# Moving pairwise products between SBUF partitions: 0/1 matmuls or DMA, in a recommendation tower on one core

## The chip, the cores and the metric

The kernel runs on one core of one Trainium2 chip. The metric is the device time of one execution in microseconds, and less is better. Besides it there is a profile of one execution, with its own time.

## The reference

For 512 samples there are 27 feature vectors of 128 numbers: the given bottom output and 26 rows looked up in embedding tables by `ids`. The 351 dot products of all pairs of features, with the bottom output behind them, go through three layers:

```python
e = jnp.stack([tbl_0[ids[:, 0]], ..., tbl_25[ids[:, 25]]], axis=1)
all_emb = jnp.concatenate([bottom_output[:, None, :], e], axis=1)
gram = jnp.einsum('bfd,bgd->bfg', all_emb, all_emb)
z = gram[:, _TRIU_I, _TRIU_J]                       # 351 pairs of a sample
h = jnp.concatenate([z, r_bottom_output], axis=1)   # 479 columns
h = jnp.maximum(h @ W_top1 + b_top1, 0.0)           # 512 columns
h = jnp.maximum(h @ W_top2 + b_top2, 0.0)           # 256 columns
return h @ W_top3                                   # one number a sample
```

All is fp32. The kernel gets that accuracy from matmuls of a high and a low part of each operand, so a product costs three matmuls: high by high, high by low, low by high.

## The kernel before, in words

The samples are four tiles of 128. Instructions are put on each engine by hand, in a written order, and engines wait for one another by semaphores alone. There is no planner: the order of calls at the end of each engine's function is the order of its work.

Up to about 53 us nine small tables are looked up by matmuls with one-hot rows (lines 653 to 675). Rows of the other 17 tables are gathered by POOL with indirect DMA (line 283), five "banks" of up to four features for each tile, into `emb`, which holds two tiles. TensorE turns a bank with four transposes (`transpose_bank`, line 531); VectorE and ScalarE in turn copy it from PSUM into `embT` (`copy_bank`, lines 293 and 409).

For a tile t the work then is this:

- `gram(t, half)` (line 545): for each half of the tile 64 small matmuls, one for each sample, which are 128 in the trace, since an fp32 matmul of this kind takes two passes; four samples stand side by side on 32 PSUM partitions each. A sample's 26 columns of products land in `pG`.
- `copy_rows` (line 216): ScalarE copies the first half, VectorE the second, into `rows`. Here the partition is 32 times the sample's place among four, plus the feature; along a partition lie the other feature and 32 groups of samples.
- `turn(t)` (line 560): layer 1 wants pairs on partitions and samples along the row. Ten turns (`TURNS`, line 34) pack the triangle of pairs into three tiles of 127 rows, and for each of four sample groups a matmul with a 0/1 matrix `sel` moves the rows of one turn to their partitions: 40 matmuls by the code, 80 in the trace. The result is in PSUM and `products(t)` (line 210) names it.
- `high_products` (ScalarE, line 444) and `low_products` (VectorE, line 296) split it into `prod_hi` and `prod_lo`.
- `layer1_bottom` and `layer1_products` (lines 569, 570, 577): three matmuls for the bottom output and nine for the products; `relu` (line 459), `transpose_h1` (line 623), `high_h1` and `low_h1` (lines 466, 296), `layer2` (lines 634, 569, 570, 577), and `layer3` on VectorE (line 331).

`products(t)` of all tiles shares one `prod_hi` and one `prod_lo`, so the next tile's split waits for `s_l1`, the end of the layer 1 before. `rows`, `pG` and `emb` have two places each. TensorE's written order weaves tile t's layers with tile t+1's transposes and gram, so that something can run while ScalarE and VectorE copy. Tile 3 comes last and has its layer 1 in two parts.

SP issues all table and weight loads (lines 230, 236, 247), then waits for `s_y` and writes the output (line 265).

Of the kernel before, what the change touches and what calls it, by code (L numbers as in the profile page):

```python
# [33 lines left out]
TURNS = [(range(24 - 3 * n, 27 - 3 * n), 0, 26 - 3 * n, n if n < 4 else 7 - n, 0 if n < 4 else 32 - 26 + 3 * n - 1)  # L34
         for n in range(8)] + [(range(1, 3), 0, 1, 0, 31), (range(2, 3), 1, 1, 1, 31)]
LAST_TURN = {j: n for n, (_, _, _, j, _) in enumerate(TURNS)}
BIAS_QUADRANT, BIAS_ROW = 3, 31
N1, N2 = 512, 256
K2 = N1 // 128
# [28 lines left out]
def tower(nc, bottom, ids, hot_ids, tables, w1, w2, b2, w3, out):  # L68
# [4 lines left out]
    with ctx:  # L73
        def sb(name, shape, dt=fp32):
            return ctx.enter_context(nc.sbuf_tensor(name, shape, dt))
# [4 lines left out]
        def sem(name):  # L80
            return ctx.enter_context(nc.semaphore(name))
# [17 lines left out]
        bot_lo = sb("bot_lo", [128, TILES, 128], fp32r)  # L99
        sel = sb("sel", [128, len(TURNS), 4, 32])  # L100
        rows = sb("rows", [128, 2, COLS, GROUPS])
        prod_hi = sb("prod_hi", [128, KTILES, 128], fp32r)
        prod_lo = sb("prod_lo", [128, KTILES, 128], fp32r)
        w_hi = sb("w_hi", [128, CHUNKS, N1], fp32r)
# [34 lines left out]
        s_sel0 = sem("s_sel0")  # L139
        s_sel = sem("s_sel")  # L140
        s_prod1 = sem("s_prod1")
        s_row = [[sem(f"s_row{t}_{k}") for k in range(len(BANKS))] for t in range(TILES)]
        s_tabhi = sem("s_tabhi")
        s_tablo = sem("s_tablo")
# [64 lines left out]

        def products(t):  # L210

            return pG[t % 2][:, 0, 0:KTILES * 128].rearrange("r (k p) -> r k p", p=128)

        def copy_rows(copy, t, half):
# [11 lines left out]
        @block.sync  # L226
        def _(sp):
            def load_table(i, p0, p1, k0, k1, loaded):

                sp.dma_start(tab[p0:p1, i % RING, k0:k1, :], tables[LOOKED_UP[i]].rearrange(  # L230
                    "(p k) d -> p k d", k=VK)[p0:p1, k0:k1, :]).then_inc(loaded, 16)

            def load_lookup(i):
                if i >= RING:
                    sp.wait_ge(s_look, (i - RING + 1) * VK)
                sp.dma_start(hot[:, i % RING, :], hot_ids[i:i + 1, :].broadcast_to([128, B])).then_inc(s_hotids[i], 16)
                load_table(i, 0, VP_MAIN, 0, VK, s_tab[i])
                load_table(i, VP_MAIN, VP, 0, VK, s_tab[i])

            def load_weights(c):  # L240
                sp.wait_ge(s_look, (LOOKED - RING + c // 2 + 1) * VK)
                if c <= KTILES:
                    dst, src = chunk(c), w1[:, c, :]
                else:
                    dst = chunk(c).rearrange("p (k n) -> p k n", n=N2)
                    src = w2.rearrange("(k p) n -> p k n", p=128)[:, 2 * (c - KTILES - 1):2 * (c - KTILES), :]
                sp.dma_start(dst, src).then_inc(s_w[c], 16)

            sp.dma_start(idx[:, :], ids.rearrange("(p t) f -> p (t f)", t=TILES)).then_inc(s_ids, 16)
# [12 lines left out]
            for c in range(CHUNKS):  # L262
                load_weights(c)
            sp.wait_ge(s_y, TILES)
            sp.dma_start(out.rearrange("(p t) o -> p (t o)", t=TILES), y[:, :]).then_inc(s_out, 16)
            sp.wait_ge(s_out, 16)
# [22 lines left out]
        def _(dve):  # L289
# [8 lines left out]
            def low_products(t, part=None):  # L298
                ks = slice(0, KTILES) if part is None else (slice(0, 1), slice(1, KTILES))[part]
                if t > 0:  # L300
                    dve.wait_ge(s_l1, t)
                else:
                    dve.wait_ge(s_prod1, 2)

                dve.wait_ge(s_phi, t + 1 if part is None else t + 2)
                subtract(prod_lo[0:127, ks, :], products(t)[0:127, ks, :], prod_hi[0:127, ks, :]).then_inc(s_plo, 1)

            def second_rows(t):
                dve.wait_ge(s_gram, 2 * t + 2)
                if t >= 2:  # L310
                    dve.wait_ge(s_turn, t - 1)
                copy_rows(nc.vector.tensor_copy, t, 1).then_inc(s_rowsv, 1)

            def low_weights(c0, c1):
# [21 lines left out]
            nc.vector.memset(ones[:, :], 1.0).then_inc(s_ones, 1)  # L336
            nc.vector.memset(embT_flat[:, TILES * 128 * FEATURES:], 0.0).then_inc(s_pad, 1)
            nc.vector.memset(prod_lo[:, :, :].bitcast(fp32), 0.0).then_inc(s_prod1, 1)
            nc.vector.memset(sel[:, :, :, :], 0.0).then_inc(s_sel0, 1)
            dve.wait_ge(s_row0, 1)  # L340
            nc.vector.tensor_copy(row0f[:, :], row0[:, :]).then_inc(s_row0f, 1)
# [31 lines left out]
            subtract(b2_lo[:, :], b2s[:, :], b2_hi[:, :]).then_inc(s_b2, 1)  # L373

            copy_bank(1, 1)
            low_weights(2, 3)
            second_rows(0)
            low_weights(3, CHUNKS)
            copy_bank(1, 3)
            low_products(0)  # L380
            second_rows(1)
            low_h1(0)
            layer3(0)
            low_products(1)
            copy_bank(2, 0)
            copy_bank(2, 2)
            low_h1(1)
            copy_bank(2, 4)
            layer3(1)

            second_rows(2)
            low_products(2)
            copy_bank(3, 1)
            low_h1(2)
            layer3(2)
            copy_bank(3, 3)

            second_rows(3)
            for part in range(2):
# [5 lines left out]
        def _(act):  # L405
# [33 lines left out]
            def high_products(t, part=None):  # L439
                ks = slice(0, KTILES) if part is None else (slice(0, 1), slice(1, KTILES))[part]  # L440
                if t > 0:
                    act.wait_ge(s_l1, t)
                act.wait_ge(s_turn, t + 1)
                nc.scalar.copy(prod_hi[0:127, ks, :], products(t)[0:127, ks, :]).then_inc(s_phi, 1)  # L444

            def first_rows(t):
                act.wait_ge(s_gram, 2 * t + 1)
                if t >= 2:
                    act.wait_ge(s_turn, t - 1)
                copy_rows(nc.scalar.copy, t, 0).then_inc(s_rowsa, 1)  # L450

            def relu(t, halves=(0, 1)):
# [36 lines left out]
            high_weights(2, 3)  # L489
            first_rows(0)  # L490
            high_weights(3, CHUNKS)
            copy_bank(1, 2)
            act.wait_ge(s_prod1, 2)
            high_products(0)
            copy_bank(1, 4)
            first_rows(1)
            relu(0)
            high_h1(0)
            high_products(1)
            copy_bank(2, 1)  # L500
            relu(1)
            high_h1(1)
            copy_bank(2, 3)

            first_rows(2)
            copy_bank(3, 0)
            high_products(2)
            relu(2)
            high_h1(2)
            copy_bank(3, 2)  # L510
            copy_bank(3, 4)

            first_rows(3)
# [7 lines left out]
        def _(pe):  # L521
# [28 lines left out]

            def turn(t):

                if t == 0:
                    pe.wait_ge(s_sel, len(TURNS))
                pe.wait_ge(s_rowsa, t + 1)
                pe.wait_ge(s_rowsv, t + 1)
                for s in range(4):
# [52 lines left out]
                          lambda k: pe.wait_ge(s_plo, parts_to(t, k))).then_inc(s_l1, 1)  # L610

            def layer1_products(t):
                for part in h1_parts(t):
                    layer1_high(t, part)
                    layer1_low(t, part)

            def transpose_h1(t, halves=(0, 1)):

# [61 lines left out]
            pe.wait_ge(s_pad, 1)  # L680
            gram(0, 0)
            transpose_bank(1, 2)
            gram(0, 1, [0])
            layer1_bottom(0)
            gram(0, 1, [1])
            transpose_bank(1, 3)
            turn(0)
            transpose_bank(1, 4)
            whole, = h1_parts(0)
            layer1_high(0, whole, 0, 1)  # L690
            gram(1, 0, [0])
            layer1_high(0, whole, 1, KTILES)
            gram(1, 0, [1])
            layer1_low(0, whole)
            gram(1, 1)
            transpose_h1(0)
            turn(1)
            layer2(0)
            transpose_bank(2, 0)
            layer1_bottom(1)  # L700
            layer1_products(1)
            transpose_bank(2, 1)
            transpose_bank(2, 2)
# [79 lines left out]
```

## Time and profile before

| | us |
|---|---|
| median of 3 runs | 121.96 |
| lowest, highest | 120.78, 122.08 |
| the profiled execution | 121.23 |
| its span, from first to last instruction | 119.4 |
| TensorE busy with matmuls | 93.1 (78% of the span) |
| VectorE, ScalarE, GpSimd busy | 63.1, 62.0, 73.5 |

The times of the trace are microseconds from the span's start. PE is TensorE, PEld its weight loads, ACT ScalarE, DVE VectorE, POOL GpSimd and SP the engine that issues plain DMAs; SPq is its queue. "issue" stands for time in which an engine waited for nothing that the profile shows. L560 is line 560 of the kernel. A matmul's duration holds its way through the array, so that of one that follows another closely overlaps with it; in the chain of work each has only the time by which it carries the chain on. A share of the chain says how much of the span passed in such work; the busy share of an engine does not.

### The profile page before, as it was taken

The page shows a single profiled execution, that of the slowest core. Times are in us where ns is not written, and L with a number is a line of the kernel's source. Part 1 is how long each engine was busy: PE and PEld are TensorE (multiplying, and loading weights), DVE is VectorE, ACT ScalarE, POOL GpSimd, SP SyncE. Part 2 cuts the span into 40 slices and gives each one's busy share as a digit, 9 for nine tenths or more (in the row PEclk, how much of TensorE's full clock was granted, in tenths as well). Part 3 has the DMA queues.
Part 4 walks back from the last instruction along what each step waited for, and adds up shares of the span by engine and source line. Part 5 has one row for each costly group of instructions (what it writes and reads, how often), then busy time and mean ns, then how long its engine had stood idle before and what let it go on. Part 6 is the DMA issues. An engine that isn't in the chain of part 4 may idle for free.

```text
span 119.4 us, 3938 instructions
## 1 busy us (share of the span) xinstructions
PE 93.1 (78%) x1692; PEld 74.9 (63%) x1692; DVE 63.1 (53%) x139; ACT 62.0 (52%) x90; POOL 73.5 (62%) x75
## 2 busy tenths in 40 slices
PE   0009989998999896986768976997977994499892
PEld 0007757877785675864556665976856773389771
DVE  6349894999999999438285030436020155010221
ACT  0526399999999999979602230128203145100330
POOL 3777777777777777777767777677776710000000
PEclk9999999999999999999999999999999999855999
DMA  0499978488589896555212212121121210000000
GB/s 18 153 318 260 258 187 253 159 220 255 135 250 221 170 259 212 131 171 178 63 49 62 54 49 70 45 62 48 49 71 49 58 30 0 5 5 5 0 0 1
DMA packets 6700, 13.69 MB, mean 115 GB/s; under 512 B 1926, under 2 KB 2567, under 8 KB 6684
## 3 DMA queue, kind: packets, MB, share of 16 engines
q1 hardware_dynamic: 4364, 8.73, 26.2%
q0 software_dynamic: 2176, 4.46, 14.3%
q8 instruction: 13, 0.21, 0.7%
q10 hardware_dynamic: 144, 0.26, 0.6%
q14 instruction: 3, 0.02, 0.1%
HBM read 13.44 MB, written 0.00 MB: 113 GB/s over the span
## 4 chain that ended last, share of the span: by engine, by line
PE 46%; ACT 23%; issue 16%; DMA 9%; SPq 2%; DVE 1%; ACTq 0%; DVEq 0%
PE pG L545 10%; PE pG L560 8%; DMA tab<-tbl 7%; PE pH L569 7%; ACT square L427 6%; ACT onehot L431 6%; PE pH L577 5%; PE pH L570 4%; ACT tab_hi L421 4%; PE pT L531 3%; PE pG L666 3%; ACT embT L409 3%; PE pG L662 2%; ACT embT L482 2%; PE pG L623 2%
## 5 line engine op out<-in xcount | busy, mean ns | idle before, releaser
L283 POOL DMA_INDIRECT emb<-tbl,idx x68 | 72.7, 1069 | 21.7 <-issue 19.5
L662 PE MATMUL pG<-onehot,tab_hi 125*128 125x512 f32 x72 | 21.1, 430 | 11.8 <-DVE onehot L355 8.7
L662 PEld LDWEIGHTS pG<-onehot,tab_hi 125*128 125x128 f32 x72 | 14.1, 202 | 16.6 <-ACT tab_hi L421 8.7
L355 DVE TENSOR_SCALAR onehot<-hot 125x512 fp32r<-125x512 int32 x59 | 21.8, 437 | 0.3
L666 PE MATMUL pG<-onehot,tab_lo 125*128 125x512 f32 x72 | 19.1, 410 | 0.0
L545 PE MATMUL pG<-embT 128*32 128x26 f32 x1024 | 13.1, 198 | 5.4 <-issue 4.3
L545 PEld LDWEIGHTS pG<-embT 128*32 128x32 f32 x1024 | 11.3, 115 | 8.6 <-issue 6.5
L666 PEld LDWEIGHTS pG<-onehot,tab_lo 125*128 125x128 f32 x72 | 14.5, 202 | 3.2
L409 ACT COPY embT<-pT 128x512 f32<-128x512 f32 (+1 forms) x10 | 10.6, 1062 | 10.5 <-PE pT L531 10.4
L421 ACT CAST tab_hi<-tab 125x1024 fp32r<-125x1024 f32 (+1 forms) x10 | 10.0, 996 | 6.5 <-DMA tab<-tbl 6.5
L293 DVE COPY embT<-pT 128x512 f32<-128x512 f32 (+1 forms) x10 | 10.2, 1024 | 4.7 <-PE pT L531 4.7
L296 DVE TENSOR_TENSOR tab_lo<-tab,tab_hi 125x1024 fp32r<-125x1024 f32 x9 | 11.0, 1217 | 2.7 <-ACT tab_hi L421 2.7
L531 PE MATMUL pT<-ident,emb 128*128 128x128 f32 x68 | 10.4, 275 | 2.2 <-ACT embT L409 1.3
L444 ACT CAST prod_hi<-pG 127x384 fp32r<-127x384 f32 (+2 forms) x5 | 2.0, 416 | 18.2 <-PE pG L560 16.2
L482 ACT COPY embT<-pG 128x512 f32<-128x512 f32 x9 | 10.9, 1206 | 0.7 <-PE pG L666 0.7
L560 PE MATMUL pG<-rows,sel 128*32 128x96 f32 (+2 forms) x320 | 9.3, 260 | 2.5 <-issue 1.5
L216 DVE COPY rows<-pG 128x416 f32<-128x416 f32 x4 | 2.4, 590 | 16.3 <-PE pG L545 16.3
L560 PEld LDWEIGHTS pG<-rows,sel 128*32 128x32 f32 x320 | 8.3, 119 | 3.7 <-issue 3.7
L531 PEld LDWEIGHTS pT<-ident,emb 128*128 128x128 f32 x68 | 8.0, 140 | 3.8 <-issue 2.6
L431 ACT ACTIVATE onehot<-square,ones 125x512 fp32r<-125x512 f32 x13 | 9.4, 725 | 0.4
L427 ACT ACTIVATE square<-hot,minus_k 125x512 f32<-125x512 int32 x13 | 9.4, 725 | 0.1
L296 DVE TENSOR_TENSOR prod_lo<-pG,prod_hi 127x384 fp32r<-127x384 f32 (+2 forms) x5 | 2.3, 474 | 8.6 <-ACT prod_hi L444 8.6
(70 smaller groups left out, 97.3 us busy)
## 6 DMA issues: line engine op xcount, KB each, us to landing
tab<-tbl SPq DMA_DIRECT2D x8, 448.0 KB
hot<-hot_ids SPq DMA_DIRECT2D x8, 256.0 KB, 4.3
tab<-w SPq DMA_DIRECT2D x6, 256.0 KB, 3.4
emb<-tbl,idx POOLq DMA_INDIRECT x68, 4.1
tab<-tbl SPq DMA_DIRECT2D x9, 52.0 KB
tab<-tbl SPq DMA_DIRECT2D x2, 224.0 KB, 5.5
hot<-hot_ids ACTq DMA_DIRECT2D x1, 256.0 KB, 4.9
bot<-bottom SPq DMA_DIRECT2D x1, 256.0 KB, 5.9
```

The source lines that it names most:

```text
L283: nc.gpsimd.indirect_dma_start(out=emb[:, t % 2, g - LOOKED - 1, :], out_offset=None, in_=tables[f], in_offset=bass.IndirectOffsetOnAxis(a ...
L296: return nc.vector.tensor_tensor(lo, whole, hi, ALU.subtract)
L355: nc.vector.tensor_scalar(hot_rows(i, k), hot[0:VP, i % RING, :], float(k), None, ALU.is_equal).then_inc(s_hotv, 1)
L409: nc.scalar.copy(bank_slots(t, i), bank(t, i)).then_inc(s_banka, 1)
L421: nc.scalar.copy(tab_hi[:, i % 2, k:k + step, :], tab[0:VP, i % RING, k:k + step, :]).then_inc(s_tabhi, 1)
L427: nc.scalar.activation(square[:, :], hot[0:VP, i % RING, :], ACT.Square, bias=minus_k[:, k - VK + 2:k - VK + 3]).then_inc(s_sq, 1)
L431: nc.scalar.activation(hot_rows(i, k), square[:, :], ACT.Relu, bias=ones[0:VP, 0:1], scale=-1.0).then_inc(s_hota, 1)
L531: last = nc.tensor.transpose(bank(t, i)[:, m, :], emb[:, t % 2, g - LOOKED - 1, :], ident[:, :])
L545: last = nc.tensor.matmul(gram_blocks(t)[32 * s:32 * s + 32, half, i, :], embT_flat[:, first:first + 32], embT[:, t, p, 1:FEATURES], start ...
L560: last = nc.tensor.matmul(products(t)[32 * j:32 * j + 32, 0:len(columns), 32 * s:32 * s + 32], sel[:, n, s, :], rows[:, t % 2, c:c + len(c ...
L662: nc.tensor.matmul(pG[i % 2][:, 0, :], tab_hi[:, i % 2, k, :], hot_rows(i, k), start=(k == 0), stop=False)
L666: nc.tensor.matmul(pG[i % 2][:, 0, :], tab_lo[:, i % 2, k, :], hot_rows(i, k), start=False, stop=(k == VK - 1)).then_inc(s_look, 1)
```

## The change

For tiles 0 to 2 (`t < LAST`) the products go to layer 1's rows by DMA. A new SBUF tile `prod` with two places, set to zero once at the start, receives them; `products(t)` names it in place of PSUM. SP issues the transfers of a tile when both halves of `rows` are copied, and for tile 2 also when the place in `prod` is free. One transfer carries one turn of one sample group: up to 26 partitions, 3 columns on each, and 32 numbers (128 bytes) in one run.

```diff
+MOVED = 16 * 4 * len(TURNS)
...
+        prod = sb("prod", [128, 2, KTILES, 128])
...
         def products(t):
 
+            if t < LAST:
+                return prod[:, t % 2, :, :]
             return pG[t % 2][:, 0, 0:KTILES * 128].rearrange("r (k p) -> r k p", p=128)
...
+            def move_products(t):
+
+                if t == 0:
+                    sp.wait_ge(s_prod0, 1)
+                elif t >= 2:
+                    sp.wait_ge(s_phi, t - 1)
+                    sp.wait_ge(s_plo, t - 1)
+                sp.wait_ge(s_rowsa, t + 1)
+                sp.wait_ge(s_rowsv, t + 1)
+                for columns, feature, features, j, row in TURNS:
+                    c = columns[0] - 1
+                    for s in range(4):
+                        sp.dma_start(prod[32 * j + row:32 * j + row + features, t % 2, 0:len(columns), 32 * s:32 * s + 32],
+                                     rows[32 * s + feature:32 * s + feature + features, t % 2, c:c + len(columns), :]
+                                     ).then_inc(s_moved[t], 16)
...
             for c in range(CHUNKS):
                 load_weights(c)
+            for t in range(LAST):
+                move_products(t)
             sp.wait_ge(s_y, TILES)
```

The features of the ten turns, that is the partitions of a transfer, are 26, 23, 20, 17, 14, 11, 8, 5, 1 and 1; the columns are 3, but 2 and 1 in the last two turns.

`high_products(t)` and `low_products(t)` wait for all 40 transfers of the tile (`s_moved[t]`) in place of `s_turn`; `first_rows` and `second_rows` of tile t wait for the transfers of tile t-2. `turn` is left for tile 3 alone.

The orders of three engines are new. TensorE's, with what left it and what came:

```diff
             gram(0, 0)
             transpose_bank(1, 2)
-            gram(0, 1, [0])
+            gram(0, 1)
+            transpose_bank(1, 3)
+            transpose_bank(1, 4)
             layer1_bottom(0)
-            gram(0, 1, [1])
-            transpose_bank(1, 3)
-            turn(0)
-            transpose_bank(1, 4)
-            whole, = h1_parts(0)
-            layer1_high(0, whole, 0, 1)
-            gram(1, 0, [0])
-            layer1_high(0, whole, 1, KTILES)
-            gram(1, 0, [1])
-            layer1_low(0, whole)
+            gram(1, 0)
+            transpose_bank(2, 0)
             gram(1, 1)
+            transpose_bank(2, 1)
+            layer1_products(0)
+            transpose_bank(2, 2)
             transpose_h1(0)
-            turn(1)
+            layer1_bottom(1)
             layer2(0)
-            transpose_bank(2, 0)
-            layer1_bottom(1)
             layer1_products(1)
-            transpose_bank(2, 1)
-            transpose_bank(2, 2)
+            transpose_bank(2, 3)
             transpose_h1(1)
-            transpose_bank(2, 3)
             transpose_bank(2, 4)
...
             gram(2, 1)
+            layer1_bottom(2)
             transpose_bank(3, 0)
-            turn(2)
-            layer1_bottom(2)
+            transpose_bank(3, 1)
             layer1_products(2)
-            transpose_bank(3, 1)
+            transpose_bank(3, 2)
             transpose_h1(2)
-            layer2(2)
-            transpose_bank(3, 2)
             transpose_bank(3, 3)
             transpose_bank(3, 4)
 
             gram(3, 0)
-            gram(3, 1)
+            layer2_high(2, 0)
+            gram(3, 1, [0])
+            layer2_high(2, 1)
+            layer2_low(2, 0)
+            layer2_low(2, 1)
+            gram(3, 1, [1])
             layer1_bottom(3)
             turn(3)
```

ScalarE's and VectorE's orders follow it: bank copies of tile 2 come earlier, the splits of tiles 0 and 1 come later, and in tile 2 one bank copy of each engine has changed places with `high_h1(2)` or with `low_products(2)` and `layer3(2)`.

## Rows read from the trace of the kernel before

**Rows 1.** The page's chain that ended last, by engine and line.

```profile
PE 46%; ACT 23%; issue 16%; DMA 9%; SPq 2%; DVE 1%; ACTq 0%; DVEq 0%
PE pG L545 10%; PE pG L560 8%; DMA tab<-tbl 7%; PE pH L569 7%; ACT square L427 6%; ACT onehot L431 6%; PE pH L577 5%; PE pH L570 4%; ACT tab_hi L421 4%; PE pT L531 3%; PE pG L666 3%; ACT embT L409 3%; PE pG L662 2%; ACT embT L482 2%; PE pG L623 2%
```

**Rows 2.** Chain in order of time (start, us, what): turns 0, 1, 3.

```profile
61.61 1.91 PE pG L560 x65
...
71.90 1.00 issue
...
108.17 2.98 PE pG L560 x61
```

**Rows 3.** Waits of SP's queue: us in total, times, longest.

```profile
SPq L265 <- DVE h2w L331: 64.9, 1, 64.9
```

**Rows 4.** SP's timeline (start, us, issue): 13-row table piece, bias, output.

```profile
2.95 0.44 SPq L230 DMA_DIRECT2D tab<-tbl  x1
...
7.91 0.25 SPq L258 DMA_DIRECT2D b2s<-b  x1
...
117.60 0.36 SPq L265 DMA_DIRECT2D out<-y  x1
```

**Rows 5.** SP's line 230, table issues: ns least, median, most; starts.

```profile
L230 SPq DMA_DIRECT2D tab<-tbl x19: 318/429/1143, 2.5 to 39.6; - x19
```

**Rows 6.** DMA tenths, 40 slices: 0.40 us of output, 0.70 of ids; landing.

```profile
DMA  0247746435544423111000000000000000000000
...
DMA  0002345285659589975465421110000000000000
...
out<-y SPq DMA_DIRECT2D x1, 2.0 KB, 1.4
```

**Rows 7.** Timeline: part of gram(0, 1), and VectorE's copy of it.

```profile
57.44 0.93 PE L545 MATMUL pG<-embT 128*32 128x26 f32 x59 [1.38 <-issue]
...
60.24 0.59 DVE L216 COPY rows<-pG 128x416 f32<-128x416 f32 x1 [2.63 <-PE pG L545]
```

**Rows 8.** Chain in order of time: tile 1's layer 1 to tile 2's rows.

```profile
77.45 0.23 PE pH L569
...
79.52 0.45 PE pT L531 x4
...
89.10 0.60 DVE rows L216
```

**Rows 9.** Windows of 1 us: length, TensorE busy, granted clock, DMA share, GB/s.

```profile
104.00:105.00 1.00, 0.23 (x17) 0.50 0.00 0
...
110.00:111.00 1.00, 1.00 (x39) 0.83 0.00 0
```

**Rows 10.** Chain in order of time: gram 3 and layer1_bottom(3).

```profile
101.41 1.34 PE pG L545 x84
102.75 2.01 issue
...
107.10 0.21 PE pH L570
```

**Rows 11.** Timeline of ScalarE and VectorE after layer 1 of tile 2.

```profile
95.53 0.66 ACT L459 ACTIVATE h<-pH 128x256 f32<-128x256 f32 x2 [2.46 <-PE pH L577]
...
96.44 0.65 ACT L466 CAST h1T_hi<-pG 128x256 fp32r<-128x256 f32 x2 [0.25 <-PE pG L623]
...
99.64 1.17 DVE L293 COPY embT<-pT 128x512 f32<-128x512 f32 x1 [0.44 <-PE pT L531]
```

**Rows 12.** Timeline of VectorE at the start.

```profile
1.10 0.38 DVE L338 MEMSET prod_lo<- 128x384 f32 x1
...
7.59 0.49 DVE L350 TENSOR_SCALAR hot<-hot,row0f 125x512 int32<-125x512 int32 x1 [3.66 <-DMA hot<-hot_ids]
```

**Rows 13.** POOL's line 283, the gathers: ns, first and last start; landing.

```profile
L283 POOL DMA_INDIRECT emb<-tbl,idx x68: 940/947/1889, 2.8 to 95.0; - x68
...
DMA to landing us min/median/max: 2.4/4.1/7.7
```

More of the change, by code:

```diff
@@ L141, in tower @@
         s_prod1 = sem("s_prod1")
+        s_prod0 = sem("s_prod0")
+        s_moved = [sem(f"s_moved{t}") for t in range(LAST)]
         s_row = [[sem(f"s_row{t}_{k}") for k in range(len(BANKS))] for t in range(TILES)]
@@ L303, in low_products @@
                     dve.wait_ge(s_prod1, 2)
+                if t < LAST:
+                    dve.wait_ge(s_moved[t], MOVED)
                 dve.wait_ge(s_phi, t + 1 if part is None else t + 2)
@@ L310, in second_rows @@
                 if t >= 2:
-                    dve.wait_ge(s_turn, t - 1)
+                    dve.wait_ge(s_moved[t - 2], MOVED)
                 copy_rows(nc.vector.tensor_copy, t, 1).then_inc(s_rowsv, 1)
@@ L338, in _ @@
             nc.vector.memset(prod_lo[:, :, :].bitcast(fp32), 0.0).then_inc(s_prod1, 1)
+            nc.vector.memset(prod[:, :, :, :], 0.0).then_inc(s_prod0, 1)
             nc.vector.memset(sel[:, :, :, :], 0.0).then_inc(s_sel0, 1)
@@ L375, in _ @@
             copy_bank(1, 1)
-            low_weights(2, 3)
             second_rows(0)
-            low_weights(3, CHUNKS)
+            low_weights(2, 4)
             copy_bank(1, 3)
+            low_weights(4, CHUNKS)
+            copy_bank(2, 0)
+            second_rows(1)
             low_products(0)
-            second_rows(1)
+            copy_bank(2, 2)
             low_h1(0)
+            low_products(1)
             layer3(0)
-            low_products(1)
-            copy_bank(2, 0)
-            copy_bank(2, 2)
             low_h1(1)
@@ L391, in _ @@
             second_rows(2)
+            copy_bank(3, 1)
             low_products(2)
-            copy_bank(3, 1)
             low_h1(2)
+            copy_bank(3, 3)
             layer3(2)
-            copy_bank(3, 3)
             second_rows(3)
@@ L442, in high_products @@
                     act.wait_ge(s_l1, t)
-                act.wait_ge(s_turn, t + 1)
+                if t < LAST:
+                    act.wait_ge(s_moved[t], MOVED)
+                else:
+                    act.wait_ge(s_turn, 1)
                 nc.scalar.copy(prod_hi[0:127, ks, :], products(t)[0:127, ks, :]).then_inc(s_phi, 1)
@@ L448, in first_rows @@
                 if t >= 2:
-                    act.wait_ge(s_turn, t - 1)
+                    act.wait_ge(s_moved[t - 2], MOVED)
                 copy_rows(nc.scalar.copy, t, 0).then_inc(s_rowsa, 1)
@@ L488, in _ @@
             copy_bank(1, 0)
-            high_weights(2, 3)
             first_rows(0)
-            high_weights(3, CHUNKS)
+            high_weights(2, 4)
             copy_bank(1, 2)
+            copy_bank(1, 4)
+            high_weights(4, CHUNKS)
+            first_rows(1)
+            copy_bank(2, 1)
             act.wait_ge(s_prod1, 2)
             high_products(0)
-            copy_bank(1, 4)
-            first_rows(1)
             relu(0)
@@ L499, in _ @@
             high_products(1)
-            copy_bank(2, 1)
             relu(1)
+            copy_bank(2, 3)
             high_h1(1)
-            copy_bank(2, 3)
             first_rows(2)
@@ L508, in _ @@
             relu(2)
+            copy_bank(3, 2)
             high_h1(2)
-            copy_bank(3, 2)
             copy_bank(3, 4)
@@ L551, in turn @@
             def turn(t):
-                if t == 0:
-                    pe.wait_ge(s_sel, len(TURNS))
+                pe.wait_ge(s_sel, len(TURNS))
                 pe.wait_ge(s_rowsa, t + 1)
@@ L612, in layer1_products @@
             def layer1_products(t):
-                for part in h1_parts(t):
-                    layer1_high(t, part)
-                    layer1_low(t, part)
+                whole, = h1_parts(t)
+                layer1_high(t, whole)
+                layer1_low(t, whole)
             def transpose_h1(t, halves=(0, 1)):
```

## Prediction

> **What bounds the kernel now.** I read the busy shares first: no engine is full (TensorE, the fullest, 78% of the span). The page's chain says why: it is TensorE for 46%, ScalarE for 23% and "issue" for 16% [rows 1]. From the end of the lookups on, the time is one thread of dependent work through TensorE, and an instruction costs time only where it stands on that thread. The 0/1 matmuls of line 560 do: the page's chain gives them 8% [rows 1], and in the chain in order of time tile 0's whole turn stands at 61.61, tile 1's has a stall of 1.00 within it, and tile 3's takes 2.98 [rows 2]. The profiled execution took 121.23 us: 119.4 of span and 1.83 around it. The median of the runs is 121.96, 0.6% more. I sum against 121.23. The runs shown spread over 1.1%, so about 1% is what a measurement of this kernel can tell from no change.
>
> Then I looked at the engine that gets the new work. SP issues nothing after the weights: it sits 64.9 us in front of the output [rows 3]. Its queue is free, and the question is how fast it can issue 40 transfers per tile.
>
> **What goes.** Three turns of 80 matmuls leave TensorE. 8% of the span is some 9.2 us; tile 3's 2.98 stays, so 6.2 go, and with the stall within tile 1's turn 7.2.
>
> **What comes: 120 transfers on one queue.** A tile's rows leave in 10 turns times 4 groups of samples, 40 transfers, issued on SP one behind the other. Before has no SBUF-to-SBUF transfer, so I bound the issue by the rows of others. A 13-row piece of a table took SP 0.44 us; the 19 table transfers have a median of 0.43 and, where SP was pushed back, a longest of 1.14; the output, 16 bytes in each of 128 rows, took 0.36; the one-row bias, the cheapest, 0.25 [rows 4, 5]. Size hardly matters: 448 KB at the median and the output's 2 KB are less than a fifth apart. The ends are thus 0.25 and 1.14. I take 0.44, the 13-row piece, because the moves too are a few rows in separate runs. A move holds SP for 40 x 0.44 = 17.6 us (10.0 and 45.6 at the ends), three of them for 52.8.
>
> The other part of a move is its landing. The output landed 1.4 us after its issue [rows 6]; I add 1.4 once per move, since the 40 overlap.
>
> The Trainium skill speaks against the change in general ("DMA: Bandwidth & Descriptors", section "Rules for kernel authors"): many small transfers should be made one, since under 64 KB one pays mostly overhead. By the fixed cost of about 2.0 us per transfer that the same page gives ("Anatomy of one DMA", an estimate here) the landing would be 2.0 where I have 1.4, 1.2 us more over the two landings that stand on the thread below; nothing else would change.
>
> **The thread of after, step by step.** (1) `gram(0,1)` is now issued undivided. Its 59 matmuls after the stall of 1.38 us began at 57.44 and took 0.93 with the tail of the last; 64 more came after `layer1_bottom(0)`. At their pace 123 end near 58.9. VectorE's copy ended at 60.83 before; it ends now at some 59.7 [rows 7].
> (2) SP issues move 0 from 59.7 to 77.3. Tile 1's rows are there long before that (its gram is some 3 us of TensorE), so move 1 follows at once, to 94.9, and has landed at 96.3. TensorE has the bank transposes, tile 1's gram and tile 0's layers 1 and 2 in this stretch, some 12 us of work for 36: it waits for move 0 from about 66 to 79, and again for move 1. So tile 0's work is beside the thread, which is now SP's queue. Behind the waits stand, in TensorE's queue, everything from `layer1_products(0)` on; in ScalarE's behind `high_products(0)` the relu and `high_h1`; in VectorE's behind `low_products(0)` bank copies and `low_h1`. SP holds the output back behind the moves, at no cost, since it needs tile 3. POOL's gathers wait only for transposes that are done by then.
> (3) ScalarE's `high_products(1)`, 0.48: 96.8. From the first product matmul of tile 1 (77.45) to the copied rows of tile 2 (89.70) the thread took 12.3 us [rows 8]. Two banks' transposes, 0.45 each, have moved ahead: -0.9. Against it stands the clock. After TensorE's stall of 2.01 us at 102.75 the granted clock went to 0.50, that is 1.2 GHz [rows 9, 10], and it was still below full between 110 and 111 although TensorE had been busy again from 104.8; there a 256-column matmul took 0.21, as long as a 512-column one at full clock (0.23) [rows 8, 10]. TensorE now comes out of waits of ten us, so I let layer 1's nine 512-column matmuls take 0.43 instead of 0.23: +1.9. That makes 13.3, and tile 2's rows at 110.1.
> (4) Move 2 needs these rows: 110.1 + 17.6 + 1.4 = 129.1, and 129.6 with `high_products(2)`. Nothing covers it: `layer1_bottom(2)` and two banks' transposes are under 2 us.
> (5) Layer 1 of tile 2 at the low clock, 9 x 0.43 = 3.9: 133.5. Then, in the new order, what gram 3 waits for: relu 0.66, ScalarE's bank copy (as long as VectorE's, 1.17), `high_h1` 0.65, the last half of `low_h1` 0.4, VectorE's bank copy 1.17 [rows 11], with handing over 4.4: 137.9. Gram 3 with layer 2 of tile 2 inside and `layer1_bottom(3)`: 2.8 + 1.9 + 0.8 = 5.5, against 6.8 from 101.41 to 108.17 before [rows 2, 10], where a stall of 2.01 stood. Turn 3 begins at 143.4, takes 1.9 at full clock as tile 0's did [rows 2]: 145.3. From the end of turn 3 (111.15) to the end of the span there were 8.2: 153.5. With 1.8 around it: 155.3.
>
> In short, the time is 102.5 us plus three times the length of a move. All of the loss is there.
>
> Costed at nothing: VectorE's memset of `prod`, 768 columns where 384 took 0.38, ahead of a wait of 3.66 us for the first ids [rows 12]; without that cover 0.8. Stalls of the instruction stream (1.38, 2.01) I leave out behind the long waits, in which the stream can run ahead; each that stays costs up to 2.
>
> **Rivals.**
> *Cheaper issue.* If a small move costs SP what the bias did, 0.25, a move is 10.0 and the time 132.5. For it: the bias is the smallest transfer. Against it: the 2 KB output, hardly larger, took 0.36.
> *The transfer engines set the pace.* A move's transfer is up to 78 runs of 128 bytes. Suppose that a transfer is shared out only in equal numbers of rows: 26 rows then use 13 engines, but 23 or 17 rows go to one, and the first engine gets 6+69+6+51+3+3+3+3+1+1 = 146 runs for each group of samples, 584 and 40 completions per tile. The output's nine packets on each engine took some 0.19 us, 21 ns each (19 busy slices of 10 ns), the ids' nine of up to 416 bytes some 0.42, 47 ns (24 slices of 17.5) [rows 6]. That is 13 to 29 us per move: at the low end below SP's 17.6 and without effect, at the high end 102.5 + 87 = 190. That SP was pushed back once, to 1.14 [rows 5], speaks for it; that this was among bulk loads, against it. The Trainium skill has such a sharing ("DMA: Bandwidth & Descriptors", "Why a DMA increments its semaphore by 16 and not by 1"): the number of engines must divide the number of rows. No row of this case shows it.
> *Not slower: the moves hide.* The mechanism is an issue that costs SP next to nothing, so that only the landing counts; the sum breaks even at (121.2 - 102.5) / 120 = 0.156 us per transfer. Well below that the turns' 7.2 us leave the thread, until the gathers bound it: the last is issued at 95.0 and the shortest landing is 2.4 [rows 13], so with transposing and copying gram 3 could begin at some 98.5 instead of 101.41, 2.9 earlier, and with the 1.3 of step 5 the time is 117.0. For it: 64.9 us of idle SP. Against it: every issue row is 0.25 or more. The Trainium skill has a sentence for it ("DMA: Bandwidth & Descriptors", "Issuing engines are not separate DMA queues"): the sequencer's time to start a DMA is usually small beside the DMA. The trace disagrees for small ones, 0.36 beside 1.4 for the output.
>
> **How the numbers follow.** The forecast (0.36 to 0.52 us per transfer, 146 to 165): 0.6. Cheaper issue (below 146): 0.15. The engines set the pace (above 165): 0.2. Not slower: 0.05, of it 0.04 faster by over 1% and 0.01 within 1%; slower is thus 0.95. The likeliest time is 155.3. Eight in ten: from 140 (0.31 us per transfer, between bias and output) to 183 (27 us per move, near the engines' high end), with some 0.1 left out on each side.
>
> **What would show it.** Right: SP's timeline is an unbroken run of 80 issues from about 60 to 95 and one of 40 from about 110 to 128, at some 0.44 each; TensorE has waits of some ten us ahead of layer 1 of tiles 0, 1 and 2, the last over 15, and the granted clock falls in them; the last issue of a move lands within 2 us. Wrong: issues of 0.15 or less, or landings long after the last issue (then the engines). If the moves have the length I say and the rest is not near 102.5, the thread is misread.

## The result, and the profile after

Before took 121.63 us in the median of 4 runs (120.78 to 122.08), after 196.79 (194.96 to 197.63): a ratio of 1.617, 95% interval 1.602 to 1.632. The prediction had the sign and the place; its 155.3 us is 41.5 short and its range ended at 183. The profiled execution took 197.63 us, 195.8 of it span. Ratios with an interval, here and below, compare only those executions of a kernel that lie within 1.5% of its fastest, so they can differ from the ratio of the medians beside them.

The page of after: busy times, two lines of its 40 slices (4.9 us each), and the chain that ended last by engine and by line. Line 267 issues the new transfers. Lines 474 (`high_products`), 575 (`gram`), 589 (`turn`), 598, 599 and 606 (the matmuls of a layer) are before's 444, 545, 560, 569, 570 and 577.

```profile
span 195.8 us, 3580 instructions
PE 92.7 (47%) x1452; PEld 72.6 (37%) x1452; DVE 64.0 (33%) x140; ACT 61.7 (31%) x90; POOL 74.1 (38%) x75
PE   0197999898946740000880000697200000475894
PEclk9999999999999995555596555589955555589999
...
SPq 44%; PE 21%; ACT 14%; issue 13%; DMA 5%; DVE 2%; ACTq 0%; DVEq 0%
SPq L267 44%; PE pG L575 4%; ACT square L454 4%; ACT onehot L458 4%; PE pH L598 3%; PE pG L691 3%; DMA hot<-hot_ids 3%; PE pG L695 3%; PE pH L606 2%; PE pH L599 2%; ACT tab_hi L448 2%; DMA prod<-rows 2%; ACT embT L436 1%; ACT embT L512 1%; PE pG L589 1%
```

Set beside [rows 1], SP's queue has come from 2% to 44% of the chain, TensorE has gone from 46% to 21%. TensorE is as busy as it was (92.7 us, 93.1 before), but the slices show three holes in it, and in each the granted clock falls to half.

The line of the transfers (ns least, median, most; first and last start), and SP's timeline (start, us):

```profile
L267 SPq DMA_DIRECT2D prod<-rows x120: 505/728/1056, 60.5 to 166.9; - x120
```
```profile
60.51 107.02 SPq L267 DMA_DIRECT2D prod<-rows  x120
193.99 0.36 SPq L289 DMA_DIRECT2D out<-y  x1
```

The median issue is 0.73 us where I had 0.44; the output after them takes 0.36 as in [rows 4], so the queue as such has not become slower. No issue of the moves is as short as the price that I gave all of them. The waits (total, times, longest) have the other side of it:

```profile
ACT prod_hi L474 <- DMA prod<-rows: 73.5, 3, 29.7
```

The chain in order of time, third move and what follows (`rows` L222 is the copy before it; starts and us):

```profile
136.53 0.60 DVE rows L222
137.22 0.93 SPq L267
...
139.11 0.82 SPq L267
...
142.23 0.62 SPq L267
...
145.26 0.77 SPq L267
...
151.38 0.81 SPq L267
...
166.31 0.59 SPq L267
166.94 1.69 DMA prod<-rows
168.71 0.52 ACT prod_hi L474
...
169.28 0.80 PE pH L598
170.07 0.43 PE pH L599
...
177.22 1.29 PE pG L575 x82
...
179.78 1.25 issue
...
183.52 0.95 issue
...
185.63 1.92 PE pG L589 x65
```

This is the form forecast: copied rows, 40 issues back to back (the first begins at 137.22, the last at 166.94), one landing of 1.69 from the start of the last issue, the split, layer 1 at the low clock (0.43 for a 512-column matmul), gram 3, turn 3. The issues are what is longer by far. The two "issue" rows near the end are stretches in which TensorE stood still and the profile shows no wait; I take them for stalls of its instruction stream. The one of [rows 10] I had left out of the sum.

### The profile page after: what moved, and what is told of

Same layout as the page of the kernel before. It is cut to its first block, busy times and chain, and to the rows that moved or that the text cites. A ratio compares the mean times of both kernels' runs of the same rounds, so it can differ in the third digit from the quotient of the medians.

```text
span 195.8 us, 3580 instructions
## 1 busy us (share of the span) xinstructions
PE 92.7 (47%) x1452; PEld 72.6 (37%) x1452; DVE 64.0 (33%) x140; ACT 61.7 (31%) x90; POOL 74.1 (38%) x75
## 4 chain that ended last, share of the span: by engine, by line
SPq 44%; PE 21%; ACT 14%; issue 13%; DMA 5%; DVE 2%; ACTq 0%; DVEq 0%
SPq L267 44%; PE pG L575 4%; ACT square L454 4%; ACT onehot L458 4%; PE pH L598 3%; PE pG L691 3%; DMA hot<-hot_ids 3%; PE pG L695 3%; PE pH L606 2%; PE pH L599 2%; ACT tab_hi L448 2%; DMA prod<-rows 2%; ACT embT L436 1%; ACT embT L512 1%; PE pG L589 1%
## 5 line engine op out<-in xcount | busy, mean ns | idle before, releaser
L598 PE MATMUL pH<-w_hi,prod_hi 128*128 128x512 f32 (+1 forms) x12 | 7.1, 596 | 75.8 <-ACT prod_hi L474 75.8
L598 PEld LDWEIGHTS pH<-w_hi,prod_hi 128*128 128x128 f32 x12 | 3.4, 284 | 77.2 <-ACT prod_hi L474 76.6
L320 DVE TENSOR_TENSOR prod_lo<-prod,prod_hi 127x384 fp32r<-127x384 f32 x3 | 1.7, 559 | 75.2 <-ACT prod_hi L474 75.2
L474 ACT CAST prod_hi<-prod 127x384 fp32r<-127x384 f32 x3 | 1.5, 511 | 73.5 <-DMA prod<-rows 73.5
L575 PE MATMUL pG<-embT 128*32 128x26 f32 x1024 | 15.7, 194 | 9.3 <-issue 6.3
L695 PE MATMUL pG<-onehot,tab_lo 125*128 125x512 f32 x72 | 18.0, 391 | 0.0
L575 PEld LDWEIGHTS pG<-embT 128*32 128x32 f32 x1024 | 12.5, 109 | 13.2 <-issue 9.2
L695 PEld LDWEIGHTS pG<-onehot,tab_lo 125*128 125x128 f32 x72 | 13.7, 190 | 2.9
L561 PEld LDWEIGHTS pT<-ident,emb 128*128 128x128 f32 x68 | 8.6, 148 | 2.7 <-issue 1.4
L320 DVE TENSOR_TENSOR h1T_lo<-pG,h1T_hi 128x256 fp32r<-128x256 f32 x8 | 3.1, 421 | 14.0 <-ACT h1T_hi L496 14.0
```

Of the source, the lines that this page charges most:

```text
L320: return nc.vector.tensor_tensor(lo, whole, hi, ALU.subtract)
L561: last = nc.tensor.transpose(bank(t, i)[:, m, :], emb[:, t % 2, g - LOOKED - 1, :], ident[:, :])
L575: last = nc.tensor.matmul(gram_blocks(t)[32 * s:32 * s + 32, half, i, :], embT_flat[:, first:first + 32], embT[:, t, p, 1:FEATURES], start ...
L598: nc.tensor.matmul(psum, a_hi[:, k, :], b_hi[:, k, :], start=start and k == 0, stop=False)
L695: nc.tensor.matmul(pG[i % 2][:, 0, :], tab_lo[:, i % 2, k, :], hot_rows(i, k), start=False, stop=(k == VK - 1)).then_inc(s_look, 1)
```

## The experiments

Besides the theory of the prediction (the time is a constant plus three times the issues of a move), three rivals were open: the transfer engines hold SP back, the runs within a row cost, or the new order of the engines costs. Extra transfers whose data nobody reads ("probes") were put into before where SP is idle, four of each form one behind the other. Each kernel with probes, and each variant of the changed kernel (e1, e2, e6, e7), was run once. Before was run again beside each series: its medians are 120.92, 121.01 and 120.76, and 123.03 for the single run beside p3_turns; single executions lie between 118.36 and 124.46.

### p1_forms: what makes an issue dear

```diff
+            sp.wait_ge(s_bot, 16)
+            for r in range(PROBE_REPS):
+                sp.dma_start(scr[0:26, 0, r // 2, :, r % 2, :],
+                             bot[0:26, 0, 0:96].rearrange("p (k g) -> p k g", g=32)).then_inc(s_probe, 16)
...
             sp.wait_ge(s_y, TILES)
```

> The kernel before, with 40 extra transfers on SP in its idle time after the weights: ten forms, four of each, into a scratch tile nobody reads. Theory 1 (an issue is SP's own work, its price set by the transfer's form): each form has one price from its first transfer on, 26 rows of three 128-byte runs cost 0.8 us as in the changed kernel, one single run 0.55; if the three-run form is what costs, one 384-byte run a row comes to 0.45 like the 13-row table piece, from SBUF or from HBM; if SBUF as the source is what costs, 26 rows from HBM come to 0.45 in either form. Theory 2 (SP is pushed back by the transfer engines): the first transfers of all are cheap, 0.45 or less, 23 rows (which go to one engine by equal parts) are the dearest, above 1, and 16 or 128 rows the cheapest. Both: the time is that of before, within 1%, since SP waits there for the output.

SP's lines (ns least, median, most). In order: SBUF to SBUF with 26 rows in 3 runs, 26 in one run, 23 and 16 in 3; HBM to SBUF with 26 rows in 3 runs; SBUF to SBUF with one row, and with 128 in 3 runs.

```profile
L272 SPq DMA_DIRECT2D scr<-bot x4: 832/871/1032, 53.2 to 56.0; - x4
L276 SPq DMA_DIRECT2D scr<-bot x4: 743/790/1271, 56.9 to 59.4; - x4
L280 SPq DMA_DIRECT2D scr<-bot x4: 625/678/722, 60.7 to 62.9; - x4
L284 SPq DMA_DIRECT2D scr<-bot x4: 608/649/1553, 63.6 to 65.6; - x4
L288 SPq DMA_DIRECT2D scr<-bottom x4: 363/378/565, 67.2 to 68.6; - x4
...
L296 SPq DMA_DIRECT2D scr<-bot x4: 589/592/595, 71.7 to 73.6; - x4
L300 SPq DMA_DIRECT2D scr<-bot x4: 630/643/1462, 74.3 to 77.2; - x4
```

The same 26 rows in the same runs cost 0.378 us from HBM and 0.871 from SBUF. A single run saves a tenth; 128 rows cost less than 26. That is the failed step in one pair of lines: for 26 rows with one end in HBM, as in every row that I had, 0.44 would have been about right.

The time was 126.84, not within 1% of before's 120.92; the two other kernels with probes were longer too (p2_ends 128.78 beside 121.01, p3_turns 126.05 beside 123.03). The trace of p1_forms has stalls of 1.38 us at 56.43 and of 2.13 at 62.30, a granted clock of 0.50 between 58 and 60, and a turn 0 of 3.30 us instead of 1.91 [rows 2]. Why the clock fell here and not in before, which has the stall of 1.38 too [rows 7], was not settled, nor whether the probes are the cause of the longer times.

### e1_two_queues: half of the issues on ScalarE's queue

```diff
-                move_products(t)
+                move_products(sp, t, (0, 1))
...
             copy_bank(2, 1)
+            move_products(act, 0, (2, 3))
             act.wait_ge(s_prod1, 2)
```

(and ahead of `high_products(1)` and `high_products(2)`)

> The changed kernel, with the transfers of two of the four sample groups issued by ScalarE, ahead of its high_products, and two by SP. Theory 1 (an issue is the issuing engine's own work): a move takes 15 us on each queue in place of 30, two moves and the third follow as before, and ScalarE's second half starts some 8 us late, behind tile 0: some 160 us. Theory 2 (the transfer engines hold SP back): the engines get the same runs, a move stays at 30, 195 us or more, and the issues on each queue take twice as long.

172.17 us. The two queues' lines:

```profile
L232 SPq DMA_DIRECT2D prod<-rows x60: 541/762/1042, 59.7 to 140.1; - x60
L232 ACTq DMA_DIRECT2D prod<-rows x60: 532/778/1527, 70.8 to 141.2; - x60
```

Each queue pays nearly the single queue's price (0.76 and 0.78 where one alone had 0.73), also where both issue at once, as in the third move: the issue is work of the issuing engine and not a place in a shared line of transfers. If the transfer engines had set the pace, two queues would have waited longer each. Of the 12 us above the expectation most are ScalarE's starts: its first 20 issues begin at 70.76, behind a bank copy that it had in its order, 11 us after SP's; its second at 94.86, behind tile 0.

### e2_one_run: one run for each row

```diff
-        prod = sb("prod", [128, 2, KTILES, 128])
+        prod = sb("prod", [128, 2, 4, KTILES, 32])
...
-                        sp.dma_start(prod[32 * j + row:32 * j + row + features, t % 2, 0:len(columns), 32 * s:32 * s + 32],
+                        sp.dma_start(prod[32 * j + row:32 * j + row + features, t % 2, s, 0:len(columns), :],
```

> The changed kernel with prod laid out by sample group, so that each row of a transfer is one run of up to 384 bytes instead of three of 128; the same bytes and the same 120 transfers. Theory 1 with the form's runs as what costs: an issue falls to 0.45, a move to 18, the time to 107 + 54 = 161. Theory 1 with something else as what costs (SBUF as source, the row count): the time stays at 195 to 198. Theory 2: a third of the runs, a move of 10 to 15, 137 to 152.

189.47 us; the median issue went from 0.728 to 0.668.

```profile
L267 SPq DMA_DIRECT2D prod<-rows x120: 519/668/927, 59.1 to 158.6; - x120
```

With a third of the runs an issue loses 0.06 us, 7.2 over 120, about the 7.3 that the time fell by from the median of after (its four runs spread over 2.7). The time lies between the expected 161 and 195: runs have a part, but a small one.

### e4_order: the new orders with matmul turns

```diff
             gram(1, 1)
+            turn(0)
             transpose_bank(2, 1)
...
             layer1_bottom(1)
+            turn(1)
             layer2(0)
...
             layer1_bottom(2)
+            turn(2)
             transpose_bank(3, 0)
```

(and no moves; the places of the turns are mine)

> The three engines' orders of the changed kernel, with no transfers: the products of tiles 0 to 2 go by 0/1 matmuls again, turn(0) ahead of the transposes of bank (2,1), turn(1) ahead of layer 2 of tile 0, turn(2) ahead of those of bank (3,0). If the whole loss is that of the moves: within 3 us of before, 118 to 124. If the new order has a part in the loss: over 126.

124.51 us in the median, a ratio of 1.037 (1.017 to 1.057). That is between the two branches of the expectation: with turns at these places the orders of the three engines cost some 4 us without any transfer, in spite of the tail part (e5) that they hold. ScalarE's and TensorE's timeline at tile 2:

```profile
95.58 1.17 ACT L409 COPY embT<-pT 128x512 f32<-128x512 f32 x1 [7.31 <-PE pT L531]
96.52 0.54 ACT L444 CAST prod_hi<-pG 127x384 fp32r<-127x384 f32 x1
97.12 0.50 PE L568 MATMUL pH<-w_hi,prod_hi 128*128 128x512 f32 x1 [1.14 <-ACT prod_hi L444]
```

A bank copy of 1.17 us, which waits for its transposes, stands ahead of `high_products(2)`, and layer 1 of tile 2 behind both. In before layer 1 of tile 2 had ended by 95.53 [rows 11]; here it begins at 97.12. This is not the whole of it: in the chains turn 2 itself ends at 94.96 here and at 92.49 in before. In after this bank copy costs nothing, since `high_products(2)` waits 29.7 us for the move; whether the rest of the orders costs something there was not measured.

### e5_tail and e8_tail_again: layer 2 of tile 2 inside gram 3, alone

```diff
-            layer3(2)
             copy_bank(3, 3)
+            layer3(2)
...
-            layer2(2)
...
             gram(3, 0)
-            gram(3, 1)
+            layer2_high(2, 0)
+            gram(3, 1, [0])
+            layer2_high(2, 1)
+            layer2_low(2, 0)
+            layer2_low(2, 1)
+            gram(3, 1, [1])
```

> The kernel before with one part of the change alone: layer 2 of tile 2 goes inside gram 3, so the bank transposes of tile 3 come ahead of it, and VectorE's bank copy (3,3) ahead of layer3(2). Gram 3 can begin at about 99.0 in place of 101.4, layer 2 follows 2.0 later. If the stall of TensorE's instructions at 102.75 stays: the same time within 0.5 us. If layer 2 covers it: 1 to 2 us faster, ratio 0.985 to 0.99.

117.88 us in the median of 7 runs, a ratio of 0.977 (0.972 to 0.981): more than either branch expected. The same kernel, once more in a second series:

> The kernel of e5_tail once more, for a profile of one of its usual executions (the one profiled there took 119.44 us, the six others 117.45 to 118.20). If the gain is that of the order: the ratio within 0.97 to 0.985 again, and in the trace gram 3 begins near 98.8, with turn 3 at full clock, some 1.9 us in place of 2.98, and begun about 2 us earlier than before. If it was chance of that chip: the ratio within 0.99 to 1.01.

118.8 in the median of 11 runs against 120.76, 0.9896 (0.983 to 0.996), between the two branches. It is faster both times; how much is open between 1% and 2.3%, as the intervals don't meet. The profiled executions took the longest of either series (119.44 and 121.1), so their chains show the place and not the size. e5's chain at gram 3:

```profile
101.45 1.27 issue
...
107.43 1.92 PE pG L560 x66
```

Turn 3 begins at 107.43 and takes 1.92 us, in before it begins at 108.17 and takes 2.98 [rows 2]. In e8's profile it takes 1.91 but begins at 109.10, later than in before, where 2 us earlier was expected: gram 3 begins at 100.76 there, for 98.76 in e5. That turn 3 takes some 1.9 after this order, as I had it, is borne out without the moves too.

### p2_ends: other ends, other numbers of rows

The edit is that of p1_forms with other forms, and `far` in HBM.

> The kernel before with 32 extra transfers on SP in its idle time, eight forms, four of each, to tell whether SBUF as the source or SBUF at both ends makes an issue dear (26 rows of three runs took 0.87 us from SBUF to SBUF and 0.38 from HBM to SBUF in p1_forms). Theory A (SBUF as source): SBUF to HBM of 26 rows comes to 0.8 or more. Theory B (both ends in SBUF): it comes to 0.36 to 0.42, like the output, and HBM to HBM likewise. By rows, between SBUF and SBUF: if what costs is the number of engines that the rows are shared out to, 13 rows cost as 26 do (0.87) and 24 nearly so, 32 and 2 rows are cheaper (0.65); if it is the number of rows, 13 rows lie at 0.75, 32 above 0.9 and 2 at 0.6.

SP's lines: SBUF to HBM with 26 rows; HBM to HBM with 26; SBUF to SBUF with 13; SBUF to SBUF with 24, 32 and 2 rows; HBM to SBUF with one row; all in 3 runs.

```profile
L272 SPq DMA_DIRECT2D far<-bot x4: 373/380/449, 51.7 to 53.1; - x4
L276 SPq DMA_DIRECT2D far<-bottom x4: 783/894/1024, 53.5 to 56.4; - x4
L280 SPq DMA_DIRECT2D scr<-bot x4: 832/843/911, 57.3 to 60.0; - x4
...
L288 SPq DMA_DIRECT2D scr<-bot x4: 778/782/800, 63.4 to 65.9; - x4
L292 SPq DMA_DIRECT2D scr<-bot x4: 598/615/683, 66.7 to 68.7; - x4
L296 SPq DMA_DIRECT2D scr<-bot x4: 622/633/693, 69.4 to 71.5; - x4
L300 SPq DMA_DIRECT2D scr<-bottom x4: 642/664/721, 72.2 to 74.3; - x4
```

SBUF to HBM is cheap (0.380), so SBUF as a source is not what costs. HBM to HBM is dear (0.894), so SBUF at both ends isn't either: here the theory missed. What holds in these forms is that a transfer between the two memories with 26 rows is cheap and one within a memory is dear. And it is not the number of rows: 13 cost about as much as 26 (0.843), and 32 less than 24, as the branch of the engines had it. The cheapness between the memories does not hold for other forms: from HBM to SBUF 23 rows took 0.505, and one row in three runs 0.664, more than two rows within SBUF (0.633). Why was not found.

### e7_half: half of the issues

```diff
-MOVED = 16 * 4 * len(TURNS)
+MOVED = 16 * 2 * len(TURNS)
...
-                    for s in range(4):
+                    for s in range(2):
```

The products of sample groups 2 and 3 are left at zero in tiles 0 to 2.

> The changed kernel with only sample groups 0 and 1 moved (the products of the other half of the samples are left at zero): 20 transfers a tile in place of 40, on SP alone, with nothing else changed. If the time is a constant and three times the move, as the prediction had it, with what the changed kernel showed (197.6 = 106.4 + 3 x 30.4): a move of 15.2 gives 152. If the transfer engines or the landing set the pace: a move of 15 as well, but with a landing that does not shrink. If anything else holds the thread (a cover that ends): more than 155.

152.05 us for an expected 152, at an unchanged median of 0.734 per issue:

```profile
L267 SPq DMA_DIRECT2D prod<-rows x60: 531/734/1403, 59.2 to 121.0; - x60
```

The loss goes with the number of issues. This is the formula's own test: one number was changed and the time followed. That it followed to 0.1 us in one execution is partly chance: the four runs of after spread over 2.7 us.

### e6_via_hbm: out to HBM in 4 transfers, back in 10

```diff
+                for s in range(4):
+                    sp.dma_start(far[t, :, :, s, :], rows[32 * s:32 * s + 32, t % 2, :, :]).then_inc(s_far[t], 16)
+                sp.wait_ge(s_far[t], 64)
...
-                    for s in range(4):
...
+                    sp.dma_start(prod[32 * j + row:32 * j + row + features, t % 2, 0:len(columns), :],
+                                 far[t, feature:feature + features, c:c + len(columns), :, :].rearrange("f c s g -> f c (s g)")
+                                 ).then_inc(s_moved[t], 16)
```

> The changed kernel with the moves by way of HBM: four transfers a tile write rows to a scratch tensor in HBM, laid out there by feature, column and sample, and after their landing ten transfers, one a turn, bring the products to prod with 512 bytes a column. No transfer has SBUF at both ends, and 14 stand for 40. If both ends in SBUF are what is dear: an issue of 0.36 to 0.45, from copied rows to landed products 1.4 + 5 (3,328 runs to HBM on 16 engines) + 3.7 + 2 = 12 us, and since tile 0 no longer has to wait for SP, 131 to 134 in all. If any transfer that touches small runs in SBUF is dear: 0.8 an issue, 18 us per move, above 145.

136.69 us. SP's lines and its timeline at move 0:

```profile
L266 SPq DMA_DIRECT2D far<-rows x12: 556/658/763, 58.9 to 98.2; - x12
L270 SPq DMA_DIRECT2D prod<-far x30: 244/295/628, 66.0 to 104.5; - x30
```
```profile
58.93 2.88 SPq L266 DMA_DIRECT2D far<-rows  x4
66.04 3.54 SPq L270 DMA_DIRECT2D prod<-far  x10
```

Fourteen issues take 6.4 us where 40 took 30. The 32-row transfers out cost 0.658, nearly twice what I expected from 26 rows (0.380), although they too go from one memory to the other. The move as a whole is not longer than expected, though: in the chain the second and the third take 11.8 and 10.8 us from copied rows to landed products, for an expected 12. What the run is above 131 to 134 lies elsewhere and was not traced. It stays slower than before: between the two steps the data has to land (2.67 us, and 2.42 at the end, in the chain of the third move), and a move with two such landings can't beat a turn of 1.91 us [rows 2].

### p3_turns: forms by turns

The edit is again that of p1_forms, with a transfer from SBUF and one from HBM by turns.

> The kernel before with 32 extra transfers on SP in its idle time. First SBUF to SBUF (26 rows of three runs) in turn with HBM to SBUF of the same shape, then SBUF to HBM (26 rows) in turn with SBUF to SBUF (32 rows), then one row from HBM with three runs, one row with one run, and HBM to HBM with one run a row, 26 and 32 rows. If an issue's price belongs to the transfer itself: 0.87 and 0.38 in turn, then 0.38 and 0.62, whatever stands before it; one row from HBM 0.65 with three runs as in p2_ends, HBM to HBM 0.89 with 26 rows. If the price is what the transfer before has left behind (a queue that still takes up the last one): the cheap forms become dear behind the dear ones, 0.6 or more each, and the dear ones cheaper.

SP's timeline, 26 rows each:

```profile
51.71 1.08 SPq L272 DMA_DIRECT2D scr<-bot  x1
52.83 0.55 SPq L274 DMA_DIRECT2D scr<-bottom  x1
53.43 0.89 SPq L272 DMA_DIRECT2D scr<-bot  x1
54.36 1.12 SPq L274 DMA_DIRECT2D scr<-bottom  x1
```

Neither theory holds as it stands. The dear form stays dear (0.85 and more). The cheap one, 0.378 among its like, takes 0.55 behind it twice, and 1.12 and 1.16 the two other times; from SBUF to HBM it is 0.55 to 0.56 behind the 32 rows, three times of three. So an issue also depends on the one before it, by some 0.17 us. The two issues above 1.1 need not come from that: single issues of 1.27 to 1.55 us stand among their like in the lines of p1_forms too. The other forms, in medians: one row from HBM 0.672 in three runs and 0.242 in one; HBM to HBM with one run a row 0.749 for 26 rows, 0.587 for 32. What makes the base of some 0.6 us within one memory stays open.

## Why the prediction was right and wrong

**The failed step** is in the part on the 120 transfers: "I take 0.44, the 13-row piece". The pitch of an issue in the third move is 29.7 / 39 = 0.76 us. Row count and separate runs were the likeness that I chose by; p1_forms shows that the ends count, at 26 rows by a factor of 2.3, and p2_ends has 13 rows within SBUF at 0.843 where the 13-row piece from HBM took 0.44. The upper end that I had given, 1.14, is one long issue among bulk loads [rows 5], which I took for a push-back, and held the truth by luck; my range stopped at 27 us per move, short of the 30.3 that it was. No rival had a dearer issue on SP itself: all that I gave to times above 165 stood for the transfer engines, which are not the cause.

Step by step, in us of the span, or as a length:

| step of the prediction | predicted | measured |
|---|---|---|
| (1) tile 0's rows copied | 59.7 | 60.4 |
| (2) move 0 issued (measured: start of its last issue) | 77.3 | 91.2 |
| move 1 issued (the same) | 94.9 | 121.6 |
| landing (measured: from the start of the last issue) | 1.4 | 1.69 |
| (3) first product matmul of tile 1 to tile 2's rows | 13.3 | 13.2 |
| (4) move 2, issues (measured: first start to last start) | 17.6 | 29.7 |
| (5) layer 1 of tile 2 | 3.9 | 4.1 |
| to gram 3 | 4.4 | 3.9 |
| gram 3 to turn 3 | 5.5 | 8.4 |
| turn 3 | 1.9 | 1.92 |
| end of turn 3 to end of span | 8.2 | 8.3 |

The issues of the three moves took 30.7 + 30.4 + 29.7 = 90.8 us of the thread for 52.8. That is 38.0 of the 42.3 us between 155.3 and the profiled 197.63. The rest is 106.8 where I had 102.5; 2.2 of these 4.3 are the stalls of 1.25 and 0.95 in gram 3, which I left out although [rows 10] has one in that very place. They need not be the same stalls; the wait of 31 us that ended 10 us earlier did not prevent them.

**Right:** moves 0 and 1 stand back to back on the queue, tile 0's work lies beside them, move 2 is covered by nothing, the last landing comes within 2 us, TensorE comes out of each wait at 1.2 GHz. TensorE's windows (length, busy, granted clock, DMA share, GB/s) show the last two:

```profile
107.00:122.00 15.00, 0.00 (x0) 0.50 0.03 3
152.00:167.00 15.00, 0.00 (x0) 0.50 0.03 4
172.00:173.00 1.00, 1.00 (x4) 0.50 0.00 0
173.00:174.00 1.00, 0.96 (x8) 0.99 0.00 0
```

The clock is back after 4 us of layer 1, as the +1.9 us in step (3) supposed.

The landing lies between my 1.4 and the 2.0 that I had from the Trainium skill ("DMA: Bandwidth & Descriptors", "Anatomy of one DMA"); the page gives that figure for DMAs issued by GpSimd, and these are SP's.

**The rivals.** "The transfer engines set the pace" gave 190, near the time, and is wrong: the landing is 1.69 after the start of the last issue, and e1_two_queues pays hardly more per issue with two queues at once. The engines' busy share of 0.03 in the windows above (0.06 in the first half of the third move) is a mean over 16 and could hide one full engine; but the transfers of 23 rows, which use one engine (below), are cheap to issue. "Cheaper issue" and "the moves hide" fall with 0.73. The sentence of the Trainium skill for the latter ("DMA: Bandwidth & Descriptors", section "Issuing engines are not separate DMA queues"), that starting a DMA is usually little beside the DMA, does not fit 40 in series: 0.76 each, some 30 us, before a landing of 1.69.

**A piece of the fallen rival was sound.** I had supposed that a transfer is shared out in equal numbers of rows. By the Trainium skill ("DMA: Bandwidth & Descriptors", "Why a DMA increments its semaphore by 16 and not by 1") that leaves 13 engines for 26 rows, one for 23 or 17, ten for 20, 14 for 14, 16 for 32 or 128. The packets in after's trace agree: in the third move each transfer ends with packets of 4 bytes, 13 of them for 26 rows, 10 for 20, 14, 11, 8 and 5 for 14, 11, 8 and 5 rows, and one for 23 and for 17. The ninth turn has two; the tenth has 16, since the trace holds its one row as 16 pieces of 8 bytes, and so it does in the one-row probe of p1_forms.

The prices within SBUF go with it in part. In the third move the issues settle at 0.82 us for 13 such packets, 0.81 for 14 and 11, 0.77 for 10 and 0.73 for 5, but at 0.69 for 8, 0.62 for one, 0.55 for two and 0.59 for 16. In the probes 26 and 13 rows cost 0.87 and 0.84, 24 rows 0.78, 2 rows 0.63, and 16, 32 and 128 rows 0.65, 0.62 and 0.64. So 1, 2 and 16 are cheap, 5 and 8 lie between, and 10 to 14 cost some 0.2 us more. Between the memories there is no such order: 26 rows with 13 such packets are the cheap form (0.378), 23 rows with one take 0.505. As far as the runs show, then, it is the issuing queue that pays for the sharing within a memory, and not the engines, where I had looked for it; why it does so was not shown.

**Where the 76 us come from:** 90.8 of issues and 3.4 of landings (two; that of move 0 lies beside move 1) came onto the thread, 7.2 of turns left it. The 10.6 that are still over (an estimate, by difference) would be work that now lies beside the moves, tile 0's layers above all; no run takes them apart.

## What to carry to other kernels

Price an issue from a transfer between the same two memories and with the same number of rows, behind the same kind of transfer; if the trace has none, put a few into an idle queue before building on it, for the nearest-looking row was off by a factor of 1.7. Then multiply by their number on one queue: 40 small transfers were 30 us, in place of matmuls that took 2. A run with half the count tells whether the queue is the bound.

## What the runs showed that I had not expected

- SP issued a 26-row transfer in 0.378 us from HBM to SBUF, in 0.380 the other way, but in 0.871 within SBUF and 0.894 within HBM.
- Within SBUF 128 rows are cheaper to issue (0.643) than 13 (0.843).
- A cheap issue (0.378) behind a dear one took 0.55 us in five cases of seven.
- One row from HBM to SBUF took 0.24 us in one run and 0.66 to 0.67 in three.
- The tail part that was the least of the change gains by itself, 1 to 2.3%: e5_tail and e8_tail_again are faster than both kernels.
